# A routed expert layer: tiles in the order of their tokens, and the join beside later tiles

## What is computed

```python
def _moe(x, ...):                       # x: 3584 tokens x 256
    gates = softmax(xf @ gW + gb)
    top2_scores, top2_idx = top_k(gates, 2)
    h = relu(einsum('nd,edf->enf', xf, W1) + b1)    # d = 256, f = 512, 8 experts
    y = einsum('enf,efd->end', h, W2) + b2
    return einsum('ne,end->nd', w, y)               # w: the two scores, zero elsewhere
...
return _ln(x + ff, ln2_g, ln2_b)        # x + ff, normalised over the 256 features
...
x = x + tanh(g_ffn) * ffn_layer
```

## Time and profile before

| | |
|---|---|
| median of 3 runs | 1115.9 us (1115.45 to 1116.56) |
| profiled execution | 1114.3 us, span 1111.8 us |
| busy share of the span | PE 95%, DVE 74%, ACT 63%, POOL 24% |
| mean granted clock of TensorE | 0.983 of full speed |
| DMA | 77.40 MB, mean 70 GB/s |

### The profile page before, as it was taken

One profiled execution on the slowest core, in us unless ns is written; L12 is line 12 of the kernel. 1 busy time (PEld: TensorE's weight loads), 2 busy tenths in 40 slices (PEclk: granted clock), 3 DMA queues, 4 the chain that ended last, 5 costly groups with the idle time before them and its releaser, 6 DMA issues. The chain is left out here.

```text
span 1111.8 us, 37043 instructions
## 1 busy us (share of the span) xinstructions
PE 1059.8 (95%) x13437; PEld 868.4 (78%) x13438; DVE 825.1 (74%) x2327; ACT 704.9 (63%) x1338; POOL 263.1 (24%) x372
## 2 busy tenths in 40 slices
PE   7999999999999999999999999999839999999976
PEld 5777777777877888777877777787629999999964
DVE  7667668788878888878778887878966666666646
ACT  5677777787877777877767777876623333343313
POOL 1011111312233222223212222222332222222234
PEclk9999999999999999999999999999969999999988
DMA  3232213301111211111111111002026222222147
GB/s 122 91 95 75 81 56 122 92 21 58 42 50 51 60 37 41 37 37 36 56 41 41 51 37 41 27 28 69 24 66 191 72 72 71 71 68 74 62 148 273
DMA packets 53555, 77.40 MB, mean 70 GB/s; under 512 B 10561, under 2 KB 37569, under 8 KB 53281
## 3 DMA queue, kind: packets, MB, share of 16 engines
q1 hardware_dynamic: 43392, 52.39, 16.2%
q0 software_dynamic: 6096, 15.66, 4.2%
q10 hardware_dynamic: 3920, 7.34, 2.0%
HBM read 51.32 MB, written 24.05 MB: 68 GB/s over the span
## 5 line engine op out<-in xcount | busy, mean ns | idle before, releaser
L812 ACT ACTIVATE probs<-quad 125x1792 f32<-125x1792 f32 (+1 forms) x128 | 213.3, 1666 | 22.0 <-PE quad L1359 21.6
L890 ACT ACTIVATE scored_half<-quad 112x500 bf16<-112x500 f32 (+1 forms) x256 | 132.5, 574 | 55.6 <-PE quad L1347 55.4
L1082 DVE TENSOR_REDUCE part_max<-quad 112x8 f32<-112x1000 f32 x96 | 114.8, 1196 | 43.4 <-PE quad L1347 43.1
L919 ACT ACTIVATE tile_w<-hidden_w 128x1024 f32 x63 | 66.6, 1056 | 97.6 <-PE quad L1539 91.4
L1539 PE MATMUL quad<-tile_inT,tile_w 128*128 128x128 f32 x1008 | 124.5, 277 | 0.0
L1551 PE MATMUL quad<-output_w,hiddenT 128*128 x504 | 119.3, 380 | 0.1
L1539 PEld LDWEIGHTS quad<-tile_inT,tile_w 128*128 128x128 f32 x1008 | 119.3, 194 | 0.1
L1085 DVE TENSOR_REDUCE part_max<-scored_half 112x8 f32<-112x1000 bf16 x96 | 113.6, 1184 | 0.0
L1278 DVE TENSOR_SCALAR hiddenT<-quad,hidden_b 128x128 f32<-128x128 f32 x252 | 71.1, 344 | 51.0 <-PE quad L1539 49.8
L1347 PE MATMUL quad<-kT_A,qT_A 32*112 32x125 f32 (+2 forms) x1536 | 106.2, 392 | 0.9 <-DVE r L1184 0.7
L720 POOL TENSOR_TENSOR inv_std_N<-moments_N,minus_half 112x1 f32<-112x1 f32 x32 | 17.6, 550 | 376.9 <-DVE moments_N L990 376.9
(11 more groups left out here) (224 smaller groups left out, 2008.7 us busy)
## 6 DMA issues: line engine op xcount, KB each, us to landing
ctxT<-in_ctxT_dram SPq DMA_DIRECT2D x32, 375.0 KB, 3.4
tile_in<-sent_dram SPq DMA_DIRECT2D x63, 129.0 KB, 2.1
join_in<-kept_dram SPq DMA_DIRECT2D x14, 512.0 KB, 5.4
hidden_w<-in_hidden_w_dram SPq DMA_DIRECT2D x8, 512.0 KB, 4.8
output_w<-in_output_w_dram SPq DMA_DIRECT2D x8, 512.0 KB, 6.3
x_in<-in_x_dram SPq DMA_DIRECT2D x32, 112.0 KB
x_res<-in_x_dram SPq DMA_DIRECT2D x32, 112.0 KB, 2.0
x_dram<-x_shift SPq DMA_DIRECT2D x32, 112.0 KB, 1.9
```

The lines of the kernel that those rows point to most:

```text
L812: act.activation(probs[0:rows, t.buffer("probs", step), :, :], bank_of(t, step)[0:rows, :, 0:U * T], ACT.Exp, scale=SCALE).then_inc(taken[ ...
L890: act.activation(scored_half[:, t.buffer("half", step), i * n:(i + 1) * n], bank[0:T, RT // 2 + i, 0:n], ACT.Copy).then_inc(copied[kind], 1)
L1082: dve.tensor_reduce(part_max[:, 0:RT // 2, f:f + RT], bank[0:T, 0:RT // 2, 0:KEYS].rearrange("t r (j s) -> t r j s", s=SC), AX_X, ALU.max) ...
```

## The change

1. *Order of the tiles.* `history` keeps the next free row of every expert after every item (it takes the place of `next_row`). The plan compares a tile's first row with all 256 of these values, which counts the items before the item of its first token; that count is the tile's key, with expert and number as tie-break. PE transposes the keys, DVE counts for each tile how many have a smaller key (`rank`), and makes a permutation matrix `order`; PE's two products of `tile_expert` and `tile_row` with `order` give the table, and `twice_order` takes the place of `twice_diag`.
2. *Join beside tiles.* `LATEST[n]` is the last tile, in the new order, that can hold a token of chunk n, for any routing: 12, 15, 19, 24, 27, 31, 34, 40, 43, 47, 52, 55, 59, 62. The steps of chunk n are put at the end of the turn of each engine at a fixed distance from it, by `join_steps(t.base)`: ADD on POOL at 7, LOAD on SP at 8, SQUARE (ACT) and INVERT (POOL) at 9, GAIN (DVE) and MAKE (POOL) at 10, STORE (ACT's queue) at 11. The distances past the last turn run in order behind the loop (`join_rest`). In a turn of POOL the order is ADD, INVERT, MAKE.
3. *Who joins.* POOL adds the two kept rows (`join_sum` in SBUF) in place of PE, and, for all chunks but the last two (`TAIL` = 12), adds the residual in place of DVE.
4. *Loop.* `EXPERTS` has no passes any more: all 65 turns are written out.

```diff
-EXPERTS = Plan(NT, 9, TR, {"A": 0, "B": 1, "D": 2}, ["A.x", "B.hT", "D.y"], {})
+EXPERTS = Plan(NT, NT, TR, {"A": 0, "B": 1, "D": 2}, ["A.x", "B.hT", "D.y"], {})
...
+LATEST = [min(NT, (TOP * T * -(-(n + 1) * JW * P // T) + E * (P - 1)) // P) - 1 for n in range(JT)]
+LOAD, ADD, SQUARE, INVERT, GAIN, MAKE, STORE = 8, 7, 9, 9, 10, 10, 11
+TAIL = JT - 2
...
+def chunks(turn, ahead):
+    return [n for n in range(JT) if LATEST[n] + ahead == turn]
...
+        def tiles_over(eng, last):
             for k in range(2):
-                eng.wait_ge(out_stored[k], (NT + 1 - k) // 2 * DMA)
+                eng.wait_ge(out_stored[k], (last + 2 - k) // 2 * DMA)
+        def result_of(eng, n):
+            done, first = result_made[n >= TAIL], TAIL if n >= TAIL else 0
+            eng.wait_ge(done, JW * (n - first + 1))
... SP
+                for n in chunks(turn, LOAD):
+                    k = n % JR
+                    tiles_over(sp, LATEST[n])
+                    if n >= JR:
+                        sp.wait_ge(join_added, JW * (n - JR + 1))
+                    sp.dma_start(join_in[:, k, :, :, :]..., io["kept"][n * (JW * P * TOP):(n + 1) * (JW * P * TOP), :]...
... POOL
+                for n in chunks(turn, ADD):
+                    k = n % JR
+                    pool.wait_ge(join_loaded[k], (n // JR + 1) * DMA)
...
+                    if n >= 2:
+                        pool.wait_ge(join_squared, JW * (n - 1))
+                        pool.wait_ge(join_scaled, JW * (n - 1))
+                    for i in range(JW):
+                        pool.tensor_tensor(join_sum[:, n % 2, i, 0:D], join_in[:, k, i, 0, :], join_in[:, k, i, 1, :],
+                                          ALU.add).then_inc(join_added, 1)
+                for n in chunks(turn, INVERT):
...
+                        pool.wait_ge(join_squared, JW * n + i + 1)
...
                         pool.tensor_tensor(join_inv[:, k, i:i + 1], square_mean[:, k, i:i + 1], minus_half[:, :],
                                            ALU.pow).then_inc(join_inverted, 1)
+                for n in chunks(turn, MAKE):
+                    if n >= TAIL:
+                        continue
...
+                    for i in range(JW):
+                        pool.wait_ge(join_scaled, JW * n + i + 1)
+                        pool.tensor_tensor(result[:, k, i, :], join_gain[:, n % 2, i, :], x1_in[...],
+                                           ALU.add).then_inc(result_made[False], 1)
... ACT
+                for n in chunks(turn, SQUARE):
+                    k = n % JR
+                    for i in range(JW):
+                        act.wait_ge(join_added, JW * n + i + 1)
...
+                        act.activation(join_square[:, i, :], join_sum[:, n % 2, i, :], ACT.Square, scale=D ** -0.5,
+                                       accum_out=square_mean[:, k, i:i + 1]).then_inc(join_squared, 1)
+                for n in chunks(turn, STORE):
+                    k = n % JR
+                    result_of(act, n)
+                    act.dma_start(io["out"][n * (JW * P):(n + 1) * (JW * P), :]..., result[:, k, :, :]...).then_inc(result_stored[k], DMA)
... DVE, plan
+            dve.tensor_scalar(tile_at[:, :], tile_expert[:, :], float(REGION), float(P), ALU.mult, ALU.add)
+            step(14)
+            dve.scalar_tensor_tensor(tile_start[:, :], tile_row[:, :], float(P), tile_at[:, :], ALU.mult, ALU.add)
+            dve.scalar_tensor_tensor(key_bias[:, :], tile_expert[:, :], float(-NB * P), tile_f[:, :], ALU.mult, ALU.add)
+            step(16)
+            dve.scalar_tensor_tensor(not_yet[:, :], history[:, 1:NB + 1, :]..., tile_start[:, :],
+                                     ones_f[:, 0:1].to_broadcast([P, NB * E]), ALU.is_le, ALU.mult, accum_out=items_before[:, :])
+            step(17)
+            dve.tensor_scalar(keys[:, :], items_before[:, :].to_broadcast([P, NT]), float(P), key_bias[:, :], ALU.mult, ALU.add)
...
+            dve.wait_ge(keys_turned, 1)
+            dve.scalar_tensor_tensor(earlier[0:NT, :], rows_bank[0][0:NT, 0:NT], keys[0:NT, 0:1], ones_f..., ALU.is_lt, ALU.mult,
+                                     accum_out=rank[0:NT, :]).then_inc(ordered, 1)
+            dve.scalar_tensor_tensor(target[0:NT, :], rank[0:NT, :], float(P), spill_f[0:NT, 0:1], ALU.mult, ALU.add)
+            dve.tensor_scalar(order[0:NT, :], spill_f[0:NT, :], target[0:NT, :], None, ALU.is_equal)
...
             dve.wait_ge(table_turned, 1)
-            dve.tensor_copy(table[:, :], rows_bank[0][0:1, 0:2 * NT]).then_inc(table_ready, 1)
+            dve.tensor_copy(table[:, :], rows_bank[1][0:1, 0:2 * NT]).then_inc(table_ready, 1)
... DVE, turns
+                for n in chunks(turn, GAIN):
+                    if n >= 2:
+                        result_of(dve, n - 2)
...
+                    for i in range(JW):
+                        dve.wait_ge(join_inverted, JW * n + i + 1)
+                        dve.scalar_tensor_tensor(join_gain[:, n % 2, i, :], join_sum[:, n % 2, i, 0:D], join_inv[:, k, i:i + 1], ln2_gain[:, :],
+                                                 ALU.mult, ALU.mult).then_inc(join_scaled, 1)
+                        if n >= TAIL:
...
+                            dve.tensor_tensor(result[:, k, i, :], join_gain[:, n % 2, i, :], x1_in[...], ALU.add).then_inc(result_made[True], 1)
... PE
-            pe.transpose(rows_bank[0][0:1, 0:NT], tile_expert[0:NT, :], ident[0:NT, 0:NT])
-            pe.transpose(rows_bank[0][0:1, NT:2 * NT], tile_row[0:NT, :], ident[0:NT, 0:NT]).then_inc(table_turned, 1)
+            pe.transpose(rows_bank[0][0:NT, 0:NT], keys[0:NT, :], ident[0:NT, 0:NT]).then_inc(keys_turned, 1)
+            pe.wait_ge(ordered, 3)
+            pe.wait_ge(plan_steps, PLANNED)
+            pe.matmul(rows_bank[1][0:1, 0:NT], tile_expert[0:NT, :], order[0:NT, :], start=True, stop=True)
+            pe.matmul(rows_bank[1][0:1, NT:2 * NT], tile_row[0:NT, :], order[0:NT, :], start=True, stop=True, ...).then_inc(table_turned, 1)
...
-                        for j in range(TOP):
-                            mm = pe.matmul(join_bank[k * JW + i][:, 0:D], ident[:, :], join_in[:, k, i, j, :], start=j == 0, stop=j == TOP - 1)
-                        mm.then_inc(join_added, 1)
```

More of the change, by code:

```diff
@@ L415, in build @@
         tile_want, tile_twice = sb("tile_want", [P, 1]), sb("tile_twice", [P, 1])
-        twice_diag = sb("twice_diag", [P, NT], BF16)
+        tile_at, tile_start, tile_new, twice = (sb(n, [P, 1]) for n in ("tile_at", "tile_start", "tile_new", "twice"))
+        items_before, key_bias, rank, target = (sb(n, [P, 1]) for n in ("items_before", "key_bias", "rank", "target"))
+        not_yet = sb("not_yet", [P, NB * E])
+        keys, earlier = sb("keys", [P, NT]), sb("earlier", [P, NT])
+        spill_f = sb("spill_f", [P, NT])
+        order = sb("order", [P, NT])
+        twice_order = sb("twice_order", [P, NT], BF16)
         row_is_new, spill_to = sb("row_is_new", [P, NT]), sb("spill_to", [P, NT])
@@ L559, in keys_over, with join_rest @@
             eng.wait_ge(made["B.s"], NB * ATTENTION.repeats["B.s"])
-        def experts_over(eng):
+        def tiles_over(eng, last):
             for k in range(2):
-                eng.wait_ge(out_stored[k], (NT + 1 - k) // 2 * DMA)
+                eng.wait_ge(out_stored[k], (last + 2 - k) // 2 * DMA)
+        def result_of(eng, n):
+            done, first = result_made[n >= TAIL], TAIL if n >= TAIL else 0
+            eng.wait_ge(done, JW * (n - first + 1))
+        def join_rest(steps):
+            for turn in range(EXPERTS.turns, LATEST[-1] + STORE + 1):
+                steps(turn)
         block = ctx.enter_context(nc.Block())
@@ L790, in _ @@
+            EXPERTS.run(pool, expert_turn)
+            join_rest(join_steps)
         @block.scalar
@@ new lines, in _ @@
+            step(16)
+            dve.scalar_tensor_tensor(not_yet[:, :], history[:, 1:NB + 1, :].rearrange("p n e -> p (n e)"), tile_start[:, :],
+                                     ones_f[:, 0:1].to_broadcast([P, NB * E]), ALU.is_le, ALU.mult,
+                                     accum_out=items_before[:, :]).then_inc(plan_steps, 1)
+            step(17)
+            dve.tensor_scalar(keys[:, :], items_before[:, :].to_broadcast([P, NT]), float(P), key_bias[:, :], ALU.mult,
+                              ALU.add).then_inc(plan_steps, 1)
@@ L1248, in _ @@
+            dve.scalar_tensor_tensor(tile_new[:, :], tile_row[:, :], float(P), tile_rest[:, :], ALU.mult,
                                      ALU.min).then_inc(plan_steps, 1)
[L1249 to L1253, removed]
@@ new lines, in _ @@
+            dve.wait_ge(ordered, 1)
+            dve.scalar_tensor_tensor(target[0:NT, :], rank[0:NT, :], float(P), spill_f[0:NT, 0:1], ALU.mult, ALU.add).then_inc(ordered, 1)
+            dve.wait_ge(ordered, 2)
+            dve.tensor_scalar(order[0:NT, :], spill_f[0:NT, :], target[0:NT, :], None, ALU.is_equal).then_inc(ordered, 1)
+            step(PLANNED)
```

(4 more changed lines are left out.)

152 lines of the change are left out of this document (70 added, 82 removed).

## The result

The changed kernel takes 1096.5 us in the median of 4 runs (1094.02 to 1098.27); the kernel before, run beside it, 1115.8 (1115.45 to 1116.56). The ratio is 0.9825 [0.9802, 0.9847]: 1.7% less, and its interval lies clear of 1; 1099 was forecast. The profiled execution has a span of 1093.6 us in place of 1111.8, 18.2 less.

A forecast was written before the change was run, and what follows sets the result against it. Behind the attention, TensorE was taken to bound the tile stage, with the plan ahead and the join alone behind. 1.7 + 8.0 − 26.7 = −17.0 us gave 1097.3 profiled, 1099 for a median, range 1090 to 1106.

The forecast's parts named there:

- The plan: Ahead of the tiles: the longer plan and SP's table read move the first tile load later, +1.7 us.
- The end: From the last tile_out to the end of the span: 17.4 in place of 44.1, −26.7 us.
- The stalls: Tile stage: STORE on ScalarE's queue waits for Pool's additions and delays the next tile's copies, +8.0 us (6 to 11).
- Six small ones: Stalls at the stores of chunks 1, 2, 4, 6, 8, 9: 0.2 each, 1.2 us.
- the four long ones: Stalls for chunks 0, 3, 5, 7, where the next chunk's ADD precedes MAKE: 1.7 each, 6.8 us.
- X: When Pool's MAKE ends, counted from the start of a turn's transposes: 5.12 in six turns, 6.59 in four, before additional delays.
- the cover: In a tile turn, the latest X that does not delay TensorE's first weights of the next tile: 5.0.
- rival C: Tile stage: the clock falls at the four long stalls, four times 1.8 more, 1106; chance 0.05.
- Rival A: Tile stage: all waits covered and no stall remains, −25.0, 1091; chance 0.15.
- Rival B: Beside the tiles: Pool and DVE in strict turns, Pool also waiting for DVE, stalls 14.0, 1105; chance 0.14.
- Rival D: Tile loop: TensorE stops to fetch the written-out turns as straight code, slower, above 1116; chance 0.04.
- E: End: tile stores land so late that chunks still pile up and the 44 us stay, 1116; chance 0.02.

The follow-up runs named there:

- order_only: The kernel before with only the new plan (new tile order), keeping its loop and its join at the end: 1117.4 us, ratio 1.0021.
- store_12: The changed kernel with STORE at a distance of 12 turns in place of 11, nothing else: 1089.2 us, ratio 0.9761.
- written_out_only: The kernel before with its tile loop written out in 65 turns and nothing else: 1114.7 us, ratio 1.000.
- join_at_end: The changed kernel with every chunk's join steps put behind the last tile, four turns apart: 1141.7 us, ratio 1.024.
- adds_on_dve: The changed kernel with both additions of the join on DVE and none on Pool: 1091.1 us, ratio 0.9797.
- make_first: The changed kernel with MAKE ahead of ADD and INVERT in Pool's part of the turn: 1093.4 us, ratio 0.9806.

## Why the prediction was right

*The plan.* +1.7 was forecast; +1.71 measured, and the table's own growth was 1.87 against 1.81. The term that mattered was SP's reading of the table ahead of its load, 1.1 by estimate and 1.22 in the trace. One sum in it is off: the listed steps add up to 3.79 and not to the 3.60 that lead to 825.85; 3.66 was measured, and with 3.79 and 1.1 the load moves by just the 1.7 that was forecast. order_only shows the same 4.89 without the rest of the change.

*The end.* −26.7 was forecast; −25.2 measured. The order of events was as told: Pool, not the load of chunk 13, is last, free for it 8.9 after the undelayed last tile_out (8.4 forecast), and from the last result to the end it takes 4.2 (4.1). Two sizes were off. The delay of the last tile_out was 1.71 instead of 1.1, because take_back was held 1.94 by Pool. And the store of chunk 12 left ScalarE's queue 1.6 later than put (11.2 instead of 9.6 after the undelayed tile_out): one result addition on VectorE took 0.91 in place of 0.42 beside Pool's addition, and everything ahead of it came late. The square behind it followed; store_12 takes this wait away.

*The stalls.* The mechanism was right, the size too large: +8.0 forecast, +4.9 measured, outside its bounds of 6 to 11. Six small ones of 0.2 don't exist, and the four long ones cost some 1.2 each instead of 1.7. The terms that were mis-sized stand in the turn shown above, whose transposes begin at 959.35. MAKE ends at 965.65, X = 6.30, where 6.59 and up to 0.7 more were forecast: Pool's store ended at +3.50 in place of +3.65, two additions in a row took 1.40 to 1.42 in place of 1.47, and no operation of VectorE came between. And from X to TensorE's weights it is 2.46 in place of 2.6. So the wait is 6.30 + 2.46 − 7.58 = 1.18. In the turn of chunk 0 VectorE did come between, for 0.25 of the 0.7 that was allowed: X = 6.55, wait 1.43. For the six others X is 4.95 to 4.96, inside the cover, which by 2.46 reaches to 5.12.

*The clock* stayed at 1.00 through all four stalls; rival C fell.

*Rival A* (no stall) was wrong in the changed kernel, and is what store_12 makes of it. *Rival B* had the right engines and, for three of the four stalls, the wrong direction: Pool's additions kept their length and VectorE was held. Pool gave way in few places: four of its 52 additions of the join took 0.76 to 0.93 in place of 0.71 to 0.74, two of them in the turn of chunk 0 and two at the end, where that of 1084.17 took 0.90 between two held operations of VectorE. The Trainium skill (SBUF — State Buffer, section SBUF: two separate sides) has the pair of ports held for a whole instruction while the other engine blocks. Here both engines are seen to wait. But take_back, normally 0.22, got through at 965.00, after three of Pool's four additions on end, and in the turn of chunk 0 after the first. The trace doesn't show what decides who is let in between two additions. *Rival D* (code) is excluded by written_out_only, *E* by the end.

The Trainium skill's factor of about two for an addition on GpSimd (GPSIMD Engine Reference, section Engine selection) is a little high for this one: 0.71 to 0.74, where nothing holds it, against VectorE's 0.42, 1.7 times. (The estimate of 10.3 that the prediction makes of that factor counts two additions a turn; with the four of the long turns it is 11.2, and the time 1102.)

So the forecast of −17.0 against −18.2 in the profile rests on the right mechanism, and its closeness in part on luck, since two errors were opposed: 3.1 too much in the stalls, 1.5 too little at the end, with 0.4 from ahead of the change.

## What to carry to other kernels

Work that moves beside a busy loop is paid for at the places where an in-order engine waits in it: write down for each added wait what stands behind it on that engine and until when that is covered, and put the store of a result a turn later than the result, rather than a faster engine under it. An order that allows overlap is worth nothing by itself (ratio 1.0021), and the overlap that it allows is worth 45 us to this join. When the end is made of hand-overs, look at the last chunk's queue neighbours: a store of the chunk before stood ahead of its first operation.

## What the hardware showed that was not expected

*One idle spell of TensorE of 1.9 us lowered the clock; longer ones elsewhere did not.* In join_at_end one take_back waited for a kept store that landed late. Its timeline:

```profile
1058.23 0.22 DVE L1363 SCALAR_TENSOR_TENSOR take_back<-tile_in,row_is_new,spill_to 128x1 uint32<-128x1 f32 x1 [4.88 <-DMA kept_dram<-tile_out,take_back]
...
1061.44 3.58 PE L1629 MATMUL quad<-output_w,hiddenT 128*128 x8 [1.89 <-DVE hiddenT L1351]
```

and its window there:

```profile
1056.00:1066.00 10.00, 8.11 (x44) 6.94 (x43) 5.97 (x21) 1.38 (x2) 1.93 (x2) 0.83 0.20 76
```

Behind 1.89 of idle time eight matmuls took 3.58 in place of 1.89, at a granted clock of 0.83 over the 10 us, a mixture of the two levels of 1.2 and 2.4 GHz. The idle time and the slow matmuls, 1.89 and 1.69, are nearly all of the 3.66 by which this tile stage is longer than that of order_only (243.93 and 240.27). The four stalls of the changed kernel, 0.92 to 1.23, left the clock at 1.00; so did a longer spell before the last tile of adds_on_dve, and one of 2.44 in the attention of written_out_only (granted clock 1.00 from 98 to 110 us):

```profile
1067.44 1.99 PE L1628 MATMUL quad<-output_w,hiddenT 128*128 x8 [2.17 <-DVE hiddenT L1339]
```

So the length of a spell alone doesn't sort them, and what does stays open. The late store, which was issued at 1050.19 and landed 7.9 later where the median is 2.4, lay beside four chunk loads of 512 KB that SP had issued on end:

```profile
1048.50 2.27 SPq L701 DMA_DIRECT2D join_in<-kept_dram  x4
```

That these held it up is likely; no run tries it.

*The attention ahead of the change differs from run to run by up to 9 us.* tile_row begins between 819.9 (adds_on_dve) and 829.2 (store_12), the columns "row at" above, though these two kernels have the same program up to there. Some of it begins with TensorE standing still behind the 88th of 96 matmuls, with nothing that the trace shows to wait for. In store_12:

```profile
106.87 0.60 PE L1444 MATMUL quad<-probs,values_A 125*32 125x112 f32 x8 [3.03 <-issue]
```

TensorE's idle time of that kind, over the whole attention, was 0.6 us in before and in adds_on_dve, 1.8 after, 3.4 in make_first, 4.3 in order_only and 4.6 in store_12, much in the order of their rows; in store_12 the granted clock over 100 to 150 us was 0.93 and in before 1.00. But it is not the whole of it: written_out_only had 3.1 of it, at a clock of 1.00, and its row is at 822.26, where that of before is. What TensorE waited for stays open. It is the reason why the kernels are compared here from row to end, and it may be why their medians spread more than their stages.
